# Typed pass of a graph network: the 26th gather of a block waits for chunk 20 of the sum by nodes, in place of its end

## The reference, cut to what matters

```python
W = jnp.einsum('rb,bio->rio', comp, basis)          # 64 relations, 64 x 64 each
msg = node_feats[src] * norm
seg = etype * N + dst
s = jax.ops.segment_sum(msg, seg, num_segments=R * N).reshape(R, N, -1)
h = jnp.einsum('rni,rio->no', s, W) + bias
...
y = relu(h) + relu(node_feats @ res_w.T + res_b)     # then a batch norm, x + y, a layer norm
```

## Time and profile before

| what | value |
|---|---|
| median of 3 runs | 12242.02 us (12239.88 to 12249.78) |
| the profiled execution | 12251.95 us, its span 12250.1 us |
| mean granted TensorE clock | 0.727 |
| busy: PE, DVE, ACT, POOL | 56%, 52%, 25%, 52% |
| typed pass | from about 560 to 5550 us of the span |

### The profile page before, as it was taken

How to read it: one execution, slowest core, us unless ns; L and a number is a source line. 1 busy time by engine, 2 the same in 40 slices (tenths; PEclk the granted TensorE clock), 3 DMA queues, 4 the chain that set the end, 5 groups by cost and what they waited for, 6 DMA issues and landing times. The chain is left out here.

```text
span 12250.1 us, 135724 instructions
## 1 busy us (share of the span) xinstructions
PE 6806.8 (56%) x46302; PEld 4998.2 (41%) x46302; DVE 6409.2 (52%) x6477; ACT 3120.3 (25%) x4717; POOL 6408.1 (52%) x6722
## 2 busy tenths in 40 slices
PE   9845444445444444447999994444444444444445
PEld 4322222323223222226998994333333333333334
DVE  4566666666666666663001004555555555555555
ACT  4333333333333333333000001111111111111112
POOL 4456666666666666660000004666666666666665
PEclk9966666666666666668999997666666666666667
DMA  9823223222222233236997994443334434433332
GB/s 388 340 85 96 96 87 96 92 90 96 89 94 96 86 97 96 86 97 229 392 392 305 392 391 108 96 97 95 94 94 96 96 96 96 97 94 94 95 96 67
DMA packets 471820, 1782.67 MB, mean 146 GB/s; under 512 B 176018, under 2 KB 242260, under 8 KB 350900
## 3 DMA queue, kind: packets, MB, share of 16 engines
q1 hardware_dynamic: 205620, 1135.92, 26.5%
q0 software_dynamic: 206272, 317.25, 11.7%
q10 hardware_dynamic: 59840, 328.38, 7.0%
HBM read 1206.15 MB, written 574.88 MB: 145 GB/s over the span
## 5 line engine op out<-in xcount | busy, mean ns | idle before, releaser
L1312 POOL DMA_INDIRECT big<-Pd,mt x3223 | 3040.8, 943 | 1689.7 <-issue 941.1
L553 PE MATMUL ps<-ring 128*128 128x490 bf16 x3223 | 1453.2, 532 | 2302.1 <-ACT Z L588 823.8
L474 DVE TENSOR_TENSOR ring<-ps,vw 128x2450 bf16<-128x2450 f32 x645 | 1741.4, 2700 | 731.0 <-remote 499.3
L440 POOL DMA_INDIRECT gv<-Yd,ix x1603 | 1512.1, 943 | 1033.3 <-issue 456.6
L440 POOL DMA_INDIRECT big<-Yd,ix x1620 | 1528.5, 944 | 900.8 <-issue 461.1
L553 PEld LDWEIGHTS ps<-ring 128*128 128x128 bf16 x3223 | 398.7, 124 | 3195.0 <-ACT Z L588 1087.6
L1341 DVE TENSOR_TENSOR ps<-ps,big 128x1024 f32<-128x1024 f32 x403 | 481.9, 1226 | 2215.4 <-DMA big<-Pd,mt 2198.2
L588 ACT ACTIVATE big<-ps 128x490 f32 x1603 | 931.3, 581 | 1610.5 <-PE ps L555 584.1
L588 ACT ACTIVATE Z<-ps 128x490 f32 x1620 | 941.0, 581 | 1508.6 <-remote 514.7
L1405 ACT ACTIVATE big<-ps 128x1024 bf16<-128x1024 f32 x269 | 275.2, 1023 | 3514.2 <-issue 3494.1
L1448 PE MATMUL ps<-idt,total 128*128 128x128 f32 x135 | 64.0, 474 | 1877.9 <-DVE total L1354 1218.8
(11 more groups left out here) (213 smaller groups left out, 11292.5 us busy)
## 6 DMA issues: line engine op xcount, KB each, us to landing
Yd<-big SPq DMA_DIRECT2D x196, 1024.0 KB, 8.8
Ah<-Z SPq DMA_DIRECT2D x108, 1568.0 KB
Ah<-big SPq DMA_DIRECT2D x108, 1568.0 KB
dr<-in_dstr SPq DMA_DIRECT2D x135, 1152.0 KB
big<-Ah SPq DMA_DIRECT2D x98, 1568.0 KB, 8.7
cb<-Ah ACTq DMA_DIRECT2D x98, 1568.0 KB, 8.9
cb<-Ah SPq DMA_DIRECT2D x98, 1568.0 KB, 8.8
Z<-Ah ACTq DMA_DIRECT2D x98, 1568.0 KB, 8.8
```

Of the source, the lines that this page charges most:

```text
L440: e.indirect_dma_start(gv[j][:, k, 0:64], None, table, bass.IndirectOffsetOnAxis(ap=ix[j][:, k:k + 1], axis=0)).then_inc(sm[f"g{j}"], 16)
L474: nc.vector.tensor_tensor(one[r][:, 0:m, :], bc_t(iof, m, W * NT), bc_f(vw[j][:, k], m, W * NT), ALU.is_equal)
L553: nc.tensor.matmul(PS[q][:, 0:W * NT], olo[r][:, c, :], one[r][:, c, :], start=True, stop=False)
L1312: e.indirect_dma_start(gv[j][:, k, :], None, Pd, bass.IndirectOffsetOnAxis(ap=mt[j][:, k:k + 1], axis=0)).then_inc(sm[f"g{j}"], 16)
```

## The change

PE raises a new semaphore, hs, at the 20th of the 30 matmuls of the sum. POOL's wait before k = 25 is for that mark of block b-1 in place of the end of its sum. All else stays.

```diff
+HS = 20
...
     def gpsimd(e):
         def turn(b, j, i):
...
-                    fourth, summed = reg(e, TH * b - 1), reg(e, b + 1)
+                    fourth, half = reg(e, TH * b - 1), reg(e, b)
                     for k in range(LA if last else KA):
...
                         if k == 25 and not first:
-                            e.wait_ge(sm["pe"], summed)
+                            e.wait_ge(sm["hs"], half)
                             e.sem_inc(sm["pool"], 1)
...
     def tensor(e):
...
                     for k in range(kn):
                         mm = nc.tensor.matmul(ag[j], gv[j][:, k, :], oh[:, k, :], start=(k == 0), stop=(k == kn - 1))
+                        if k == HS - 1:
+                            mm.then_inc(sm["hs"], 1)
                     mm.then_inc(sm["pe"], 1)
```

More of the change, by code:

```diff
@@ L1634, in _ @@
                 roots(e, sm, 2, st2[:, :])
-        edge_phase(["m0", "m1", "o0", "o1", "ix", "pool", "mul", "pe", "io", "pw", "pr", "vw", "acc", "pl", "cc", "zj", "ro", "rp"] + [
+        edge_phase(["m0", "m1", "o0", "o1", "ix", "pool", "mul", "pe", "io", "pw", "pr", "vw", "acc", "pl", "cc", "zj", "ro", "rp", "hs"] + [
             f"{n}{t}" for n, c in (("cm", 2), ("gb", GN)) for t in range(c)], typed_pass, "g0", "g1")
```

## The result

The changed kernel is slower: 12400.43 us (median of 4 runs, 12358.51 to 12421.72) against 12245.9 us for the kernel before (4 runs). The ratio is 1.0122, with a 95% interval of 1.0093 to 1.015. I had forecast 12012 us and given "slower" 0.29; the range held the time, the direction was wrong. The profiled execution took 12390.95 us with a span of 12389.1.

The account below looks back on a forecast made before the run. The prediction took an order of waits around POOL's two stops to bound the typed pass. An earlier release of the stop before gather 26 was to save 230 us: 12242 - 230 = 12012 us, range 11930 to 12450.

Parts of the forecast that it names:

- What bounds the kernel: Typed pass: no engine is busy over 56%; an order of waits bounds it, with two POOL stops, 46.15 us a block.
- The mark on the matmul costs nothing: New count on PE's sum matmul: costed at nothing; 108 marks could not cost more than 31 us.
- When POOL sees the new mark: POOL's wait before gather 26: three cases of the mark's delay, worth 495, 125 or 265 us; 230 us taken.
- when the passes run freely again: Case for POOL's 26th gather: mark seen as the sum's stall ends, 5.1 us a pair of blocks, 265 us.
- So up to 4.1 us can pass through.: Block's second half, from cm0 to the sum: ACT idles 5.1 us before cm0, DVE 0.97, so it can start earlier.
- 37.4 + 4.0 + about 2.1 = 43.6 us: POOL's forecast round: gathers, stop before k = 15, new stop; against 46.15 us, 2.6 us less a block.
- The third rival: Marks before cm0 are held longer in POOL's row and eat the lead: nothing changes, 12242 us, chance 0.12.
- The first rival: POOL no longer stops before gather 26 and the sum's stall goes on: slower, 12450 us, chance 0.29.
- The 4.5 us delay: Rival: new mark seen only 4.5 us after POOL's last gather: 125 us less, 12117 us, chance 0.19.
- the fourth rival: POOL never stops before gather 26 and all follows: up to 495 us less, about 11850 us, chance 0.07.
- What would make it wrong: Sign against the forecast: the sum's stall is set by something beside POOL's gathers, such as the stores of Ah.

Follow-up runs that it names:

- e10: The changed kernel with POOL's earlier stop moved from its 16th gather to its 12th, on a chip with the hold: 12295.91 us beside 12331.42.
- e12: The kernel before without POOL's stop ahead of its 26th gather, on a chip with the hold: 12551.10 us beside 12331.42.
- e18: The kernel before with POOL's earlier stop moved from its 16th gather to its 12th, on a chip with the hold: 13170.36 us beside 12321.81.
- e17: The kernel before without both POOL stops, a fill of 128x16 elements after each gather, on a chip with the hold: 13166.28 us beside 12321.81.
- e2: The changed kernel with the mark behind chunk 10 of the sum in place of chunk 20, without the hold: 10688.23 us, ratio 1.0.
- e9: The changed kernel with the mark behind chunk 10 of the sum again, on a second chip without the hold: 10690.74 us, ratio 1.0.
- e13: The changed kernel with the mark behind chunk 26 of the sum in place of chunk 20, without the hold: 10690.21 us beside 10690.46.
- e14: The kernel before with both POOL stops replaced by a wait for landed gathers ahead of every fifth gather, without the hold: 11787.93 us beside 10690.46.
- e5: The changed kernel as it is, on a chip with the hold: 12538.5 us beside 12331.07 for the kernel before.
- e11: The kernel before without POOL's stop at its 16th gather, on a chip with the hold: 13175.02 us beside 12331.42.

## Why the prediction was wrong

- **What bounds the kernel.** Right: an order of waits around POOL, with two stops. The step moved whenever a stop was moved or left out (e10 to e12, e18). But it holds on some chips only; on others the block is POOL's 37.5 us and the change is worth nothing.
- **The mark on the matmul costs nothing.** Right. On a chip without the hold, kernels that carry it take 10688 to 10691 us, as before; with the hold, e10 carries it at no loss.
- **When POOL sees the new mark.** Right: between "when the passes run freely again" and 4.5 us later, with the first nearer. The stop is 2.8 us; I had said 2 to 3.5. In the block above the sum's passes run freely from 3489.95 (a row of 19 passes), and the gather starts at 3491.00.
- **"So up to 4.1 us can pass through."** This is the step that failed. I took the stop before the 16th gather as a fixed 4.0 us that comes forward with the gathers, and checked only that ACT, DVE's group 0 and L528 were ready for an earlier cm0. I did not ask which marks come before cm0 in the same row of gathers. In the kernel before, the row begins at the sum's end and the marks up to chunk 14 pass; chunk 17's is held some 7 us, and chunk 20 is placed by the time the row lets go. Begun 3 us earlier, with a dozen passes of the sum inside it, the row holds the marks from chunk 8 on, and the chunk that POOL waits for ends 12 us later. The stop that I had at 4.0 us measures 7.8 us. The term "37.4 + 4.0 + about 2.1 = 43.6 us" should have been 37.4 + 7.8 + 2.8 = 48.0; the step measured is 47.70.
- **The third rival** ("the marks before cm0 fall later into POOL's longer row ... and DVE's group 5 and L528 eat the lead") had the mechanism and the row to look at, DVE's idle time. I priced it as the loss of the lead, 12242 us, as if the earlier marks could cost no more than they were brought forward. They cost 7.8 - 4.3 = 3.5 us of stop for 5.0 - 2.8 = 2.2 saved, 1.3 us a block net, and the step grew by 1.37.
- **The first rival** (no stop left, slower) gave a time near the result, 12450, by another way. There was a stop in all 102 blocks looked at, and the sum's stall ended about when I said, so the nearness is luck. Its mechanism, a PE that lacks instructions while POOL issues, would fit the count of matmuls and the late instructions of POOL itself in e17, but is not shown; I had looked for it in the sum only.
- **The 4.5 us delay** is not how the new mark behaves: the stop would then be 4.5 + 0.78 - 1.25 = 4.0 us, and it is 2.8. It was no fixed distance either, but the value for a row of 20 gathers.
- **A slip in the fourth rival.** "About 11850 us with half of that lost again" does not follow: 12242 less half of 495 is 11995, inside my own forecast. It did not come to bear.
- **What would make it wrong.** That the stores of Ah cause the stall is not borne out: the stall follows POOL's row when only the stops are moved (49 and 39 passes before, 28 in e10). It was not tried by itself.

Of the two pages of the Trainium skill that the prediction weighed: that a mark may be seen later than a matmul's computed end (Perfetto Trace Analysis, Tensor Engine Instruction) agrees with the traces with the hold, by 9.2 us for chunk 11. That a sequencer fetches its instructions over a DMA queue of its own (Runtime: NRT & Kernel Launch, Instruction fetch mechanics) would fit a hold that begins after a number of matmuls. The traces speak against a fetch in every block: the profile lists queues of kind "instruction", and in the kernel before they have these packets between 710 and 4450 us, two in some 80 blocks:

```profile
q8 instruction: 1, 0.02, 0.0%
q14 instruction: 1, 0.01, 0.0%
```

Unless such packets are missing from the record, what PE lacks in each block is not fetched there.

**What stays open.** Why a chip has the hold or not, and by what path POOL's gathers keep PE back. That PE's own progress starts it is read from the traces; no run changed only the number of PE's instructions. Whether a lower rate of gathers prevents it was not tested: the fills of e17 left the rate as it was. The marks at chunks 10 and 26 of the sum (e2, e9, e13) ran only where nothing is held, so how the loss grows with the lead was not measured. Short pauses inside the row (e14) were not run with the hold either; at 2.35 us each they leave little to win. The kernels with the hold were run once each behind the result, so the sizes hold to what one run can tell; e10's gain over e5 rests on two chips whose kernels before agree within 0.4 us.

## What to carry to other kernels

A wait that no data needs can still set the pace through the idle time it makes. Before moving one, list every mark that falls into the stretch of work it separates, not only the one it waits for, and ask which of them change sides, and how far the other engine has got when they do, not only how many microseconds have passed. A wait that finds its mark already raised is no stop (e18), so a pacing wait has to be checked by its idle time in the trace. And measure on more than one chip: here the effect that decides the change was absent on four chips, and its presence made the same kernel 15% slower on the others (12246 to 12331 against 10690).

## What the runs showed of the hardware that I had not expected

- Two classes of chips: 10689 to 10704 us against 12246 to 12331 us for one and the same kernel, with gathers of 0.94 us in both. With the hold, the typed pass takes 46.3 us a block, without it 37.5.
- With the hold, marks and passes of PE are late once PE has started 24 to 32 matmuls (53 to 56 where most are passes of the sum) since POOL's row of gathers began, 4 to 13 us into it. Some late marks come out inside the row (e11: chunk 17's, 13.5 us before the last gather). All is free 1.38 to 1.42 us times the number of gathers after the row's start, in rows of 10 to 30, which is 2.6 to 6.2 us after the last gather where nothing delays POOL. Without the hold, rows of gathers that never end hold none.
- With the hold, POOL itself is idle for up to 2.2 us ahead of single gathers at the end of a row of 30 gathers and 30 fills, with no wait in the trace (e17).
- A wait of POOL for the landing of its latest gather keeps it idle for 2.35 us; a fill of 128x16 elements between two gathers changes their distance by 0.005 us.
